# The attention output product in three F32R terms, its result transposed back on TensorE, and the second norm one step later

## The reference, cut to what matters

```python
# x: (B=8, S=1024, D=256) f32; H=16 heads of 16; Wk 256x256, Wv 256x1024, Wf 1024x256
K = split_heads(x @ Wk + bk);  V = split_heads(x @ Wv + bv);  Q = split_heads(x)
o = softmax(causal(Q @ K.T)) @ V            # (B, S, 1024)
x = layernorm(x + (x + gelu(o) @ Wf + bf))  # the first norm: y
gate, up = x @ wg.T, x @ wu.T               # int32 weights / 127, 256 -> 768
h = silu(gate) * up
x = layernorm(x + h @ wd.T)                 # the second norm: z
```

## Time and profile before

| | us |
|---|---|
| median of 3 runs | 1856.99 (1853.64 to 1857.23) |
| the profiled execution, own time | 1861.0 |
| its span | 1859.3 |
| TensorE matmul busy | 1769.6 (95%) |
| VectorE busy | 1401.7 (75%) |
| ScalarE busy | 1050.3 (56%) |
| GpSimd (POOL) busy | 1229.3 (66%) |
| 1024 records of the Wf product, summed | 232.1 |

### The profile page before, as it was taken

How to read it: one execution, slowest core, us unless ns; L and a number is a source line. 1 busy time by engine, 2 the same in 40 slices (tenths; PEclk the granted TensorE clock), 3 DMA queues, 4 the chain that set the end, 5 groups by cost and what they waited for, 6 DMA issues and landing times. The chain is left out here.

```text
span 1859.3 us, 37606 instructions
## 1 busy us (share of the span) xinstructions
PE 1769.6 (95%) x10304; PEld 965.2 (52%) x10304; DVE 1401.7 (75%) x3411; ACT 1050.3 (56%) x1374; POOL 1229.3 (66%) x1151
## 2 busy tenths in 40 slices
PE   6899999999999999999999999888889999999996
PEld 4444444444444444444444444333467767676763
DVE  3777777778787787777878787877467878787864
ACT  2466666566566566666666565555454656565552
POOL 3488888888888888888888888989711222222221
PEclk8999999999999999999999999999989999999998
DMA  8775656556555655656556555662476666767500
GB/s 281 210 194 164 197 141 188 166 150 194 145 172 158 190 151 162 195 138 188 164 152 191 148 173 145 190 155 74 137 178 186 163 178 170 174 172 170 170 23 23
DMA packets 261153, 303.16 MB, mean 163 GB/s; under 512 B 28241, under 2 KB 177873, under 8 KB 261073
## 3 DMA queue, kind: packets, MB, share of 16 engines
q1 hardware_dynamic: 261072, 302.19, 57.6%
HBM read 174.20 MB, written 127.93 MB: 162 GB/s over the span
## 5 line engine op out<-in xcount | busy, mean ns | idle before, releaser
L791 POOL TENSOR_TENSOR weight_sum<-weight_sum,weights 128x512 f32<-128x512 f32 (+3 forms) x448 | 736.9, 1646 | 144.1 <-DVE weight_sum L1333 106.9
L1147 ACT ACTIVATE weights<-ring 128x1024 f32<-128x1024 f32 x576 | 570.5, 1026 | 226.2 <-PE ring L835 223.3
L835 PE MATMUL o_acc<-weights,v_pair 128*64 128x512 f32 (+3 forms) x3072 | 586.1, 502 | 13.3 <-POOL weights L749 12.9
L826 POOL TENSOR_TENSOR h_lo<-hidden,h_hi 128x512 f16<-128x512 f32 x96 | 114.4, 1193 | 392.7 <-ACT h_hi L1087 392.7
L1298 DVE TENSOR_REDUCE part_max<-ring 128x2 f32<-128x1024 f32 x256 | 300.9, 1216 | 93.2 <-PE ring L835 93.1
L835 PEld LDWEIGHTS o_acc<-weights,v_pair 128*64 128x64 f32 x3072 | 188.4, 137 | 299.0 <-issue 261.4
L1307 DVE CUSTOM_DVE_ANT_0 scrap<-ring,causal 128x128 bf16<-128x128 f32 (+3 forms) x512 | 225.1, 486 | 105.9 <-PE ring L835 105.5
L1307 DVE CUSTOM_DVE_ANT_0 scrap<-ring,causal,part_max 128x256 bf16<-128x256 f32 (+3 forms) x512 | 251.3, 547 | 67.5 <-PE ring L835 67.1
L835 PE MATMUL ring<-q_stack,k_stack 50*128 50x512 f32 (+3 forms) x1536 | 266.4, 385 | 30.6 <-DVE part_max L1298 17.4
L835 PE MATMUL ring<-k_stack,q_stack 48*128 48x512 f32 (+3 forms) x1536 | 257.5, 373 | 1.7 <-DMA k_stack<-k_rows 1.6
L835 PE MATMUL ring<-wf_sb,g 128*128 128x256 f32 x1024 | 232.1, 382 | 3.9 <-DVE y_pre L1390 2.9
(11 more groups left out here) (123 smaller groups left out, 2068.5 us busy)
## 6 DMA issues: line engine op xcount, KB each, us to landing
v_pairs<-v_unit SPq DMA_DIRECT2D x64, 512.0 KB, 3.5
v_pair<-v_pairs SPq DMA_DIRECT2D x64, 512.0 KB, 5.1
o_heads<-o_pair SPq DMA_DIRECT2D x64, 512.0 KB, 3.2
g<-o_heads SPq DMA_DIRECT2D x16, 2048.0 KB, 8.2
den_wide<-reciprocals SPq DMA_DIRECT2D x32, 1024.0 KB, 13.1
q_stack<-q_rows SPq DMA_DIRECT2D x128, 192.0 KB, 3.6
k_stack<-k_rows SPq DMA_DIRECT2D x128, 192.0 KB, 4.2
q_rows<-x_hi SPq DMA_DIRECT2D x28, 512.0 KB, 3.6
```

Of the source, the lines that this page charges most:

```text
L791: pool.tensor_tensor(dst, other, weights(t), ALU.add).then_inc(s_add, 1)
L826: pool.tensor_tensor(h_lo[:, f], h32[f % 2][:], h_hi[:, f], ALU.subtract).then_inc(s_hl, 1)
L835: return nc.tensor.matmul(o, l, r, start=start, stop=stop)
L1147: nc.scalar.activation(W[i][:], bank_of("t", i)[:], ACT.Exp).then_inc(s_w, 1)
```

## The change

The Wf product is made of F32R operands: gelu(o) is split in a rounded high part and a low rest, Wf likewise, and three of the four terms are summed (high x high, high x low, low x high). Wf is now stationary (128x128 pieces) and the 512 tokens of a unit move, so that the result comes out transposed (channels by tokens), in two halves d of 128 channels. ScalarE runs Gelu twice on each chunk, once into `dn` (the memory of den_wide, read as F32R: the high part) and once in place; POOL subtracts (`g_low`, four operations of 128x1024). VectorE splits Wf once (`split_wf`). x and bf are now taken transposed; VectorE adds them to the transposed result (`y_preT`), TensorE transposes the sum back into rg[0] (`transpose_back`, eight 128x128), and statistics and `y` read it there.

In TensorE's step the order becomes: half 0 of the product, transposes of unit r-1, half 1, gate/up blocks 0 to 2, transpose back, gate/up blocks 3 to 5, down. VectorE starts a step with norms 0 to 3 of unit r+1, then y_lo, norms 4 to 7, the adds, the hidden blocks with statistics between them, y, z, z_pre; ScalarE starts with the gelus of chunks 0 to 3, then y_hi, the gelus of chunks 4 to 7, then the silus. The second norm of a unit (statistics of z_pre and z) moves one step later, so the stage has one step more. SP loads `den_wide` of unit r+2 when the product of unit r is done (before: when its norms were), and stores z one step later. Unit 0's product moves to turns 4 and 5 of the end of `attend`, behind the last denominators.

```diff
+            def wf_product(r, n, d):
+                cols = slice(P * d, P * (d + 1))
+                if d == 0 and r > 0:
+                    pe.wait_ge(s_yn, UT * n)
+                for c in range(HC):
+                    if d == 0:
+                        pe.wait_ge(s_ghi, HC * n + c + 1)
+                    for k, w in enumerate((wf_hi, wf_lo)):
+                        mm(rg[0][:, d], w[:, c, cols], dn[r % 2][:, c], c + k == 0, False)
+                for c in range(HC):
+                    if d == 0 and c % 2 == 0:
+                        pe.wait_ge(s_glo, HC // 2 * n + c // 2 + 1)
+                    e = mm(rg[0][:, d], wf_hi[:, c, cols], g[r % 2][:, c], False, c == HC - 1)
+                e.then_inc(s_wf, 1)
+            def transpose_back(r, n):
+                pe.wait_ge(s_y, DC * (n + 1))
+                for i in range(UT):
+                    for c in range(DC):
+                        e = nc.tensor.transpose(yb_ps[:, D * i + P * c:D * i + P * (c + 1)],
+                                                y_preT[:, c, P * i:P * (i + 1)], ident32[:])
+                e.then_inc(s_yb, 1)
...
             def finish(r, it):            # TensorE
+                if 1 <= r < UNITS:
+                    wf_product(r, n, 0)
+                if before:
+                    transpose_y(r - 1, n - 1)
+                if 1 <= r < UNITS:
+                    wf_product(r, n, 1)
+                if before:
+                    gate_up(r - 1, n - 1, range(0, FC // 2))
                 if r < UNITS:
-                    wf_product(r, n, (0, 1))
-                if r >= 1:
-                    transpose_y(r - 1, n - 1)
-                if r < UNITS:
-                    wf_product(r, n, (2,))
-                if r >= 1:
-                    gate_up(r - 1, n - 1)
-                if r < UNITS:
-                    wf_product(r, n, (3,))
-                if r >= 1:
+                    transpose_back(r, n)
+                if before:
+                    gate_up(r - 1, n - 1, range(FC // 2, FC))
                     down(n - 1)
...
             def gelus(r, n, slices=range(HC)):            # ScalarE
                 for c in slices:
                     act.wait_ge(s_gn, HC * n + c + 1)
-                    nc.scalar.activation(g[r % 2][:, c], g[r % 2][:, c], ACT.Gelu,
+                    nc.scalar.activation(dn[r % 2][:, c], g_in[r % 2][:, c], ACT.Gelu,
+                                         bias=bv_sb[:, c:c + 1]).then_inc(s_ghi, 1)
+                    nc.scalar.activation(g_in[r % 2][:, c], g_in[r % 2][:, c], ACT.Gelu,
                                          bias=bv_sb[:, c:c + 1]).then_inc(s_gelu, 1)
...
+                if r + 1 < UNITS:
+                    gelus(r + 1, n + 1, range(HC // 2))
+                if 1 <= r <= UNITS:
+                    act.wait_ge(s_yt, n)
                     for c in range(DC):
                         nc.scalar.activation(y_hi[:, c], rg[1][:, c], ACT.Copy,
                                              scale=YSCALE).then_inc(s_yh, 1)
+                if r + 1 < UNITS:
+                    gelus(r + 1, n + 1, range(HC // 2, HC))
...
-                if r + 1 < UNITS:
-                    gelus(r + 1, n + 1)
...
+            def split_wf():            # VectorE, turn 1 of the step behind the last scores
+                v.tensor_copy(wf_hi[:], wf_in[:]).then_inc(s_wfhi, 1)
+                dve.wait_ge(s_wfhi, 1)
+                v.tensor_tensor(wf_lo[:], wf_in[:], wf_hi[:].bitcast(F32), ALU.subtract).then_inc(s_wfs, 1)
...
             def finish(r, it):            # VectorE
+                if r + 1 < UNITS:
+                    norm(r + 1, it, range(HC // 2))
                 if f0:
                     for c in range(DC):
                         dve.wait_ge(s_yh, DC * m + c + 1)
                         v.scalar_tensor_tensor(y_lo[:, c], yt_ps[:, BANK * c:BANK * (c + 1)], YSCALE, y_hi[:, c],
                                                ALU.mult, ALU.subtract).then_inc(s_yl, 1)
+                if r + 1 < UNITS:
+                    norm(r + 1, it, range(HC // 2, HC))
...
+                    for c in range(DC):
+                        dve.wait_ge(s_x2, DC * n + c + 1)
+                        dve.wait_ge(s_wf, DC * n + c + 1)
+                        v.tensor_tensor(y_preT[:, c], rg[0][:, c], xn[r % 2][:, c], ALU.add).then_inc(s_y, 1)
...
+            def g_low(r, n):            # POOL, ahead of the h_lo of a step
+                for i in range(HC // 2):
+                    pool.wait_ge(s_gelu, HC * n + 2 * i + 2)
+                    settle(pool, s_passed["pool"])
+                    part_ = g[r % 2][:, 2 * i:2 * i + 2]
+                    pool.tensor_tensor(part_, g_in[r % 2][:, 2 * i:2 * i + 2], dn[r % 2][:, 2 * i:2 * i + 2].bitcast(F32),
+                                       ALU.subtract).then_inc(s_glo, 1)
...
             def load_dn(r, it):            # SP
-                    sp.wait_ge(s_gn, HC * (n - 1))
+                    sp.wait_ge(s_wf, DC * (n - 1))
```

## The result

The changed kernel is **slower: 1950.01 us** (median of 4 runs, 1948.29 to 1952.28) against 1857.11 beside it, ratio 1.0505 (95% interval 1.0492 to 1.0519). The page: TensorE's share of busy time is down from 95% to 91%, and its granted clock leaves full speed in the last third of the span.

A forecast was written before the change was run, and what follows sets the result against it. TensorE was taken as the bound, filling the whole 30.61 us step. Steps 2 to 14 +36, clock +11, start +18, step 15 +0.3, end -6 sum to +59: 1920 profiled, 1916 us median, range 1868 to 1948.

The forecast's parts named there:

- TensorE's own work: TensorE's step: F32R product and transposes back bring its work to 28.24 us, 2.4 us less than the period before.
- the rival's 0.27 each: Transposes back: each costs what a lone one does, 0.27 us, 13 x 1.3 us more, 1933 us; chance 0.02.
- Stall two: Gate/up block 2 waits 2.5 us for hidden block 0, behind ScalarE's 16 gelus a unit.
- Stall one: Down straight after up waits for POOL's h_lo, ending 7.87 us after up instead of 5.24: 2.6 us a step.
- D: The end of down in a step, from which the prediction counts the chain to the next hidden block.
- VectorE's chain: Statistics to z's end 6.4 us, about when down ends; then z_pre until 1.2 us after down, when the next norm starts.
- The clock: TensorE's clock may fall after block 2's wait: half of 1.67 us, 0.84 a step, 13 steps, +11 us.
- The rival "clock falls at every stall two or also in down": Clock falls at every block 2 wait (1927 us) or in down as well (up to 1948); chance 0.13.
- The start: Start of the stage: Wf split and later loads of unit 2 delay unit 0's down end by 18 us (14 to 22).
- The end: Last step: shorter wait ahead of the last transposes, only 1.2 us for z_pre, -6 us; step 15 +0.3.

The follow-up runs named there:

- Filled, with early statistics and y from SBUF: Changed kernel plus unread matmuls in TensorE's gaps, y_pre's statistics behind hidden3 and hidden4, y_pre copied from PSUM by ScalarE: 1915.53 us, ratio 1.0306.
- The fill: Changed kernel plus matmuls nobody reads, ahead of gate/up block 2 and of down's two waits for h_lo: 1926.74 us, ratio 1.0381.

## Why the prediction was right and wrong

- **TensorE's own work: right.** Product records are 0.227 us apart and the transposes back 1.04 for eight at full clock; the rival's 0.27 each was wrong. TensorE's work lost 2.4 us a step and nothing came of it.
- **Stall two: right** in place and cause: block 2 at 16.7 us behind the first norm for 16.5. Its size, 2.5 us in the mean for 2.5, agrees in part by luck: it is 3.2 us in a step with no drop of the clock ahead of it, where the norm starts 2.0 us behind down's end (1626.67 for 1624.63) and not 1.2, and 2.1 behind a drop in down. The run with one gelu, and without GpSimd's part, showed what the chain is worth: without it 31.2 us a step.
- **Stall one: right as a wait, wrong as a cost.** It is there in the size of the earlier trace rows, but with it taken away the step fell by 0.26 us. The prediction said itself that VectorE's z ends "about D" and then let down's end alone set the next norm. Where two chains end together the later one counts, and taking away the other gains nothing. Without a drop in down VectorE's is the later by 1.1 us.
- **VectorE's chain: mis-sized by 0.9 us a step, 12.1 us in all.** The prediction took 6.4 us from statistics to z's end out of the earlier trace rows and sums right behind; it is 6.9 with 0.03 to 0.13 ahead of the sums, for the most part since y now reads PSUM (1.90 us for four, z from SBUF 1.37). From up's end to the next norm are 9.9 us, not 9.07, and 0.2 more to block 2: 34.33 a step without drops, not 33.4. Filled, with early statistics and y from SBUF the step is 33.65.
- **The clock: mis-sized by 1.0 us a step, 13.1 us in all.** This is the step that failed by choice: 0.84, half of 1.67, because "none so short is seen to do it each time". It does it nearly each time: low at block 2 in 11 of 13 steps, twice as long in two of them, and in down in 8. The fill measured 1.85 us a step. The rival "clock falls at every stall two or also in down" (1927 to 1948) had the mechanism. Its price for down was too high, 0.5 us a drop, because VectorE ends together with down and the next stall two takes the rest back.
- **The start: right in sum, in part by luck.** The first unit's down ends 17.8 us later than before (1409.96 for 1392.12), for +18. The norm of unit 2 starts at 1375.84 behind the load of g, 2.2 us earlier than the 1378 said, and from there to down's end are 34.1 us, not 32.2.

```profile
1375.84 2.50 DVE L1404 TENSOR_TENSOR g_raw<-g_raw,den_wide_raw 128x512 f32<-128x512 f32 x4 [3.40 <-DMA g_raw<-o_heads]
```

- **The end: half right.** From down's end in step 15 -3.7 for -6: the transposes of the last step wait 2.03 us for z_pre, not 1.2, and the first gate/up blocks behind them again run at the lower level (granted clock 0.50 from 1917 to 1921), as they did before (0.50 from 1829 to 1833). Step 15 itself is 0.7 longer than before, for 0.3.

```profile
1913.23 1.09 PE L1076 MATMUL ring<-ident,y 128*128 128x128 f32 x8 [2.03 <-DVE z_pre L1525]
```

- **Sum.** 59 us forecast; 12.1 of VectorE's chain, 13.1 of clock and 2.7 at the end are missing: 87, the difference of the two profiled executions.

The range ended at 1948 and the time is 1950. It held the clock's upper bound but not that and an error in the chain at the same time.

## What to carry to other kernels

Before work is taken off the engine that is the bound, add up what the change puts on the others in the order in which they run: 5 us of gelu on an engine busy 58% of the time cost, with the subtraction that goes with them, 5 us a step, because they stood between a norm and the first silu. When an operand moves from SBUF to PSUM, price its readers again. When two chains end together, look for the later one before working on either, and put stretches of GpSimd where VectorE works from PSUM.

## What the hardware showed that was not expected

- One gap of 2.0 to 3.3 us per step lowered TensorE's clock in 11 of 13 steps (2.0 to 2.1 us in six of eight, 3.1 to 3.3 in five of five), where gaps of 1.33 and 0.72 us alone did so in 2 of 13; behind the larger gap in the same step the small ones were followed by a drop in 8 of 13. Unused matmuls of 0.22 us each in both places kept the clock at 1.00 and saved 1.85 us a step.
- VectorE held by GpSimd: 2.32 us for an instruction on 8 elements a partition that takes 0.17 us alone, 3.54 us for two casts that take 0.75.
